# RWKV block and cross attention on one core: first quarter mixed chunk by chunk, v's weights centred later, one signal per swap, two weights loaded later

## The reference, cut to what matters

```python
xa = _ln(x, ln1_w, ln1_b)
sx = concatenate([state[:, 1:2] - xa[:, :1], xa[:, :-1] - xa[:, 1:]], axis=1)
xxx = tanh((xa + sx * maa_x) @ maa_w1).reshape(b, l, 5, DM)      # the low rank, DM = 32
xxx = einsum('blfd,fde->blfe', xxx, maa_w2)
xm = xa[:, :, None] + sx[:, :, None] * (maa_stack + xxx)         # five mixes: k, w, v, r, g
xk, xw, xv, xr, xg = (xm[:, :, j] for j in range(5))
w = exp(-exp(time_decay + tanh(xw @ td_w1) @ td_w2))
r, k, v = xr @ Wr.T, xk @ Wk.T, xv @ Wv.T;  g = silu(xg @ Wg.T)
# a scan over the 128 steps: out = r (u * k v + s); s = k v + w * s
# per-head norm of out: subtract the mean over the head's 16 columns, divide by the deviation
x1 = x + og * g @ Wo.T                                            # then a feed-forward part
```

## Time and profile before

| | |
|---|---|
| runs | 951.91, 955.3, 957.22 us; median 955.3 us |
| profiled execution | 953.33 us, span in the trace 951.6 us |
| busy share of the span | TensorE 92%, VectorE 72%, GpSimd 56%, ScalarE 41% |
| mean granted TensorE clock | 0.965 of full speed |
| moved by DMA | 100.34 MB, 105 GB/s |

### The profile page before, as it was taken

How to read it: one execution, slowest core, us unless ns; L and a number is a source line. 1 busy time by engine, 2 the same in 40 slices (tenths; PEclk the granted TensorE clock), 3 DMA queues, 4 the chain that set the end, 5 groups by cost and what they waited for, 6 DMA issues and landing times.

```text
span 951.6 us, 10578 instructions
## 1 busy us (share of the span) xinstructions
PE 877.9 (92%) x3588; PEld 392.8 (41%) x3588; DVE 688.8 (72%) x875; ACT 388.2 (41%) x755; POOL 535.4 (56%) x573
## 2 busy tenths in 40 slices
PE   2789999999989997999899998999979999799988
PEld 1234433443434442444344444444435444444454
DVE  6336799899879996889889999779995324523442
ACT  3032323332234322213235454554446353736394
POOL 1001685888949789399789996888873101010200
PEclk8698999999979998899999999999989999999999
DMA  8082458465773639265734043446002212010101
GB/s 288 11 169 86 122 145 167 143 177 138 155 185 113 186 80 196 70 171 147 208 106 112 24 105 103 109 109 163 17 23 67 78 33 79 0 45 1 44 1 44
DMA packets 93943, 100.34 MB, mean 105 GB/s; under 512 B 22850, under 2 KB 64066, under 8 KB 91842
## 3 DMA queue, kind: packets, MB, share of 16 engines
q1 hardware_dynamic: 86978, 87.09, 36.3%
q10 hardware_dynamic: 6912, 12.59, 3.8%
HBM read 65.05 MB, written 33.55 MB: 104 GB/s over the span
## 4 chain that ended last, share of the span: by engine, by line
PE 54%; DVE 16%; POOL 10%; issue 6%; ACT 5%; DMA 4%; SPq 3%; ACTq 0%; DVEq 0%; POOLq 0%
PE PS L1359 36%; PE PS L1488 3%; DVE M L1072 3%; DVE VB L1188 3%; PE PS L1592 3%; POOL VB L755 3%; PE PS L1368 3%; POOL VB L751 2%; POOL VB L747 2%; PE PS L1426 2%; PE PS L1569 2%; DMA scr_v<-STG 2%; DVE VB L1069 2%; SPq L497 2%; PE PS L1503 1%
## 5 line engine op out<-in xcount | busy, mean ns | idle before, releaser
L1359 PE MATMUL PS<-M,W 128*128 128x512 f32 x544 | 264.4, 628 | 15.5 <-DVE M L1072 11.6
L1359 PEld LDWEIGHTS PS<-M,W 128*128 128x128 f32 x544 | 102.4, 199 | 154.2 <-issue 138.1
L747 POOL TENSOR_TENSOR VB<-KR,VB 128x1008 f32<-128x1008 f32 x64 | 129.8, 2028 | 58.0 <-PE PS L1488 53.3
L1188 DVE TENSOR_TENSOR_SCAN VB<-PS,VB 128x512 f32<-128x512 f32 x128 | 149.0, 1206 | 16.1 <-POOL VB L755 14.2
L755 POOL TENSOR_TENSOR VB<-VB 128x1008 f32<-128x1008 f32 x64 | 151.1, 2362 | 3.5
L1069 DVE TENSOR_TENSOR VB<-VB,PS 128x2048 f32<-128x2048 f32 x64 | 146.0, 2282 | 2.0
L635 POOL TENSOR_SCALAR NM<-MV 128x2 f32<-128x2 f32 (+1 forms) x24 | 5.4, 227 | 231.2 <-DVE MV L1316 141.7
L751 POOL TENSOR_TENSOR VB<-WG,VB 128x1008 f32<-128x1008 f32 x64 | 128.7, 2011 | 0.1
L1359 PE MATMUL PS<-W,M 128*128 128x512 f32 x224 | 105.7, 597 | 0.0
L1334 DVE TENSOR_REDUCE SM<-PS 128x1 f32<-128x512 f32 x64 | 43.4, 687 | 55.7 <-PE PS L1592 55.0
L1488 PE MATMUL PS<-VB,HEAD 128*32 128x512 f32 x512 | 69.7, 617 | 5.2 <-DVE VB L1069 5.0
(11 more groups left out here) (176 smaller groups left out, 1317.8 us busy)
## 6 DMA issues: line engine op xcount, KB each, us to landing
VB<-scr_vs SPq DMA_DIRECT2D x64, 256.0 KB, 7.5
W<-in_w SPq DMA_DIRECT2D x8, 1024.0 KB, 9.2
scr_vs<-STG SPq DMA_DIRECT2D x64, 64.0 KB, 5.1
scr_v<-STG SPq DMA_DIRECT2D x16, 256.0 KB, 6.3
scr_w<-STG ACTq DMA_DIRECT2D x16, 256.0 KB, 5.0
scr_k<-STG ACTq DMA_DIRECT2D x16, 256.0 KB, 2.1
KR<-scr_k SPq DMA_DIRECT2D x16, 256.0 KB, 4.2
WG<-scr_w SPq DMA_DIRECT2D x16, 256.0 KB, 5.6
```

The costliest lines, as they stand in the source:

```text
L747: po.tensor_tensor(vo, KO[:, 0:N2 - 1].unsqueeze(1).to_broadcast([P, S, N2 - 1]), VB[:, 2 + s, 0, :, 1:N2], ALU.mult).then_inc(g_kv, 1)
L1188: sc = dv.tensor_tensor_scan(s_, PS[:, 5, :], b_, 0.0, ALU.mult, ALU.add)
L1359: mm = pe.matmul(o, l, r, start=i == 0, stop=i == 3)
```

## The change

Four edits, and the five order tables written anew for them:

1. In quarter 0 `shift_a` and `first_mix` give way to `front_by_chunk`: for each chunk of 128 channels, as soon as its EXT is there, two subtractions of a quarter of the size and the chunk's first mix.
2. Centring v's weights is a stream of its own ("w", `stream_w`), which the order table puts behind the first mix.
3. Each of the four swaps has its own semaphore `d_xr[f]`, and `mix(q, f)` waits for that of its f alone.
4. The weights of r and g are loaded behind quarter 0's swaps.

```diff
-        d_xr = sem("d_xr")
+        d_xr = [sem(f"d_xr{f}") for f in range(4)]
...
-                for wi in (W_K, W_R, W_G):
-                    sp.dma_start(W[:, wi], w8[wi].rearrange("(c p) n -> p c n", p=P)).then_inc(d_w[wi], 16)
-                    yield
+                sp.dma_start(W[:, W_K], w8[W_K].rearrange("(c p) n -> p c n", p=P)).then_inc(d_w[W_K], 16)
+                yield
                 for q in range(NQ):
...
                     for f in range(4):
-                        sp.dma_start(low_rank(f, 1), low_rank(f, 0)).then_inc(d_xr, 16)
+                        sp.dma_start(low_rank(f, 1), low_rank(f, 0)).then_inc(d_xr[f], 16)
+                        yield
+                    for wi in (W_R, W_G) if q == 0 else ():
+                        sp.dma_start(W[:, wi], w8[wi].rearrange("(c p) n -> p c n", p=P)).then_inc(d_w[wi], 16)
                         yield
...
-            def centre_wv():
+            def stream_w():
...
+            def front_by_chunk():
+
+                w.wait_ge(g_col, 1)
+                sx, xa = SXS[0].rearrange("p c (b t) -> p c b t", t=L), EXTS[0][:, :, :, 1:L + 1]
+                for ec in range(C4):
+                    w.wait_ge(a_ext, ec + 1)
+                    for late, part in ((xa[:, ec, :, EVEN], ODD), (EXTS[0][:, ec, :, 0:N2], EVEN)):
+                        tt(sx[:, ec, :, part], late, xa[:, ec, :, part], ALU.subtract).then_inc(v_sub, 1)
+                    yield
+                    w.wait_ge(v_sub, 2 * (ec + 1))
+                    w.wait_ge(d_vec, 32)
+                    stt(btv(mof(0, None)[:, ec, :]), sxv(ec, 0), vec(V_MX + ec), xav(ec, 0), ALU.mult, ALU.add).then_inc(v_m1, 1)
+                    yield
...
                     if q == 0:
-                        yield from centre_wv()
-                    yield from shift_a(q)
-                    yield from first_mix(q)
+                        yield from front_by_chunk()
+                    else:
+                        yield from shift_a(q)
+                        yield from first_mix(q)
...
-                        w.wait_ge(d_xr, 64 * (q + 1))
+                        w.wait_ge(d_xr[f], 16 * (q + 1))
```

Of the order tables the first rows of one show the kind of edit:

```diff
 ORDER_DVE = (
-    "a:2 end:1 a:17 end:1 m:13 end:1 m:2 end:1 m:6 a:2 m:1 a:1 m:2 a:2 m:1 a:3 m:1 end:1 m:2 l:1 end:1 "
+    "a:16 w:5 m:13 end:1 m:4 end:1 m:4 a:2 m:2 a:4 m:1 a:1 m:1 a:1 m:5 end:2 m:2 end:2 a:6 p:1 scan:6 p:1 "
```

More of the change, by code:

```diff
@@ L1111, in first_mix @@
                 for ec in range(C4):
-                    w.wait_ge(v_sub, 2 * (q + 1))
+                    w.wait_ge(v_sub, 2 * (q + 1) + 6)
                     w.wait_ge(d_vec, 32)
@@ L1344, in stream_l @@
                     yield
-            weave(ORDER_DVE, {"a": stream_a(), "m": stream_m(), "p": stream_p(), "scan": stream_scan(), "end": stream_end(), "c": stream_c(),
+            weave(ORDER_DVE, {"a": stream_a(), "m": stream_m(), "w": stream_w(), "p": stream_p(), "scan": stream_scan(), "end": stream_end(), "c": stream_c(),
                               **{n: stream_l(i) for i, n in enumerate(LANES)}})
```

## The result

The changed kernel takes 932.56 us (median of four runs, 929.47 to 933.27), the kernel before 955.33 on the same chip: ratio 0.9759, 95% interval 0.9723 to 0.9795. Two later series, each on another chip, gave 0.9788 (0.9752 to 0.9824) and 0.9773 (0.974 to 0.9806). So it is 2.1 to 2.4% faster, some 20 to 23 us. I had said 945 us, 10 us faster, between 938 and 952: the gain was more than twice what I forecast, and outside the range. Two single executions in the experiments, of 4959 and 3072 us, stood far from all others of their kernels and are in no ratio.

A forecast was written before the change was run, and what follows sets the result against it. The prediction took TensorE, busy 92% of the span, with its holes and halved clock, as the bound. Front 8.1 plus stores 1.0 made 9.1 us off 953.3: 944.2 (946.2 from the median), stated as 945 us, range 938 to 952.

The forecast's parts named there:

- The front: Quarter 0's start: chunked first mix, later centring and swap signals let VectorE start on a mix result 8.1 us sooner (7.4 to 8.9).
- The stores of v: Ahead of the projection of k: earlier issue and faster landing of the last store gain 1.0 us, bounds 0 and 2.7.
- The weights of r and g: Loaded behind quarter 0's swaps, they should land by 32 us, in idle DMA time, at no cost.
- The clock's rival: Projections from 37.03 to 46 us at full instead of half clock: 4.5 us more gain, some 940 us; chance 0.15.
- All the rest of the five tables: Order tables beyond the priced terms: same instructions in another order, mostly by a few places; taken as 0.
- for one crowded queue: Quarter 3's store of v landing in 11.90 us: TensorE's wait plus work lost to the halved clock, priced at 11 us.
- a second such stall in quarter 1: X2's 1 MB load ahead of quarter 1's first scr_v store gives the gain back: 955 us, no change; chance 0.13.
- my sign that no hole behind 100 us would be longer than quarter 3's: TensorE, behind 100 us: no hole longer than the 6.04 us of quarter 3.
- My other sign: Quarters 1 to 3: ScalarE's longest wait for a store of v stays at or below 6.4 us.

The follow-up runs named there:

- one seam: Changed kernel with the old order tables from quarter 4's projections, near 420 us, on; against the kernel before: ratio 0.9861 (0.9826 to 0.9897).
- another run with a seam: Changed kernel with each engine's table new up to the end of quarter 2's projections and old behind; against the kernel before: ratio 1.0022 (0.9996 to 1.0048).

## Why the prediction was wrong

**The front was right.** The last first mix ended at 19.94 us (19.9 forecast), the low rank at 21.13 (21.2), the mix began at 23.94 (23.9), VectorE took its result at 26.05 (26.1). The gain at this point is 34.20 - 26.05 = 8.15 us, 8.1 forecast. The first projection gained 7.65 (37.03 to 29.38), since it now waits 0.72 us for ScalarE's WOB: rows of the weights WL were put ahead of it. The eight differences of 256 elements took 0.42 us each (417 to 425 ns) where I took 0.41; two of them overlap a little, 0.76 us from the start of the first to the end of the second. The formula of the Trainium skill, "VectorE: DVE Perf Modes", section on the trn2 errata, gives 0.42 as an estimate, and the trace agrees.

**The stores of v were mis-sized.** "I take 0.55 + 0.45 = 1.0 us": the last store of v was issued 3.18 us after its copy instead of 3.71, which is the 0.55, but it landed after 4.6 us instead of 4.24. The hole ahead of the projection of k stayed, 2.33 for 2.26 us. So this term gave 0.2 net, and the projection of k came at 63.9 and not at 62. The weights of r and g landed at 30.1 and 33.0 us, the second 1 us later than I had said, at no cost that the trace shows.

**The clock's rival did not come.** The projections of v still ran at the low level (halved clock from 24.0 to 37.6 us, before from 32.5 to 46.2). What went was another stretch, 18.9 to 25.7 us under the low rank; I had allowed for a part of it in the low rank's time.

**The step that failed** is "All the rest of the five tables: the same instructions in another order, mostly by a few places. I take 0". The edits with the old tables gave 0.9912, 8.4 us, and my sum was 9.1, so the forecast is that of the edits. With the tables it is 0.976 to 0.979, so the other rows are worth 12 to 15 us. I priced this term at nothing without going through the holes that those rows could close, and the trace of before has two large ones behind the start.

The one at quarter 2's decay (4.17 us, then 10.3 us of halved clock in which TensorE was busy for 9.87) stands in none of my sums; by the way I priced quarter 3's it is 4.17 + 4.9 = 9 us. It is here that the result's trace gains most, 10.6 us from 246 to 287, and 10.1 and 11.1 in the other two; with the edits alone it was 1.4. Up to 3.6 us of that can be the one trace of before, as said above.

The other is quarter 3's store of 11.90 us. I had priced it at 11 us "for one crowded queue", and moving four rows out of that queue in the kernel before measured 10.5 us in the trace. But I used the price only to ask whether the change makes a second such stall in quarter 1, and never asked whether the new order removes the one that is there. It does so in part: the slowest store took 9.7, 9.4 and 7.3 us in the three traces of the changed kernel, TensorE's hole of 6.04 us is gone and one of 2.40 us, for GpSimd, stands there, and the lead grows by 3.8, 5.5 and 8.8 us from 287 to 405.

The new rows also cost something that I had not priced: the wait ahead of the feed-forward's first mix is 6.72 us instead of 4.51. That is longer than 6.04, so my sign that no hole behind 100 us would be longer than quarter 3's failed. My other sign, that ScalarE's waits for a store of v stay below 6.4 us, was met, with 3.17 at most.

**What stays open.** SyncE's rows for quarter 2's stores to 440 us account for 7 of the 12 to 15 us on one chip. With SyncE's whole table old nearly all was lost (0.9899), although its rows ahead of quarter 2 counted for nothing by themselves (0.9776); the two ran on different chips, and how much of it is interplay I can't say. Which of the new rows close the hole at quarter 2's decay is open: with SyncE's old table 7.9 us of lead came there still, so the computing engines' rows have a part. SyncE's new rows over old rows of the other engines weren't tried, so what they are worth alone is open. Whether the 1 MB load of X counts (0.9992, 0.9828, 0.9875) is not settled, nor is a kernel with the four edits, the old tables and only the four rows moved, which wasn't tried: 0.9912 x 0.9845 = 0.976 is an estimate from two runs, if their gains add, no better than the changed kernel.

## What to carry to other kernels

When a change rewrites an order of work, go through every stall that the profile of before shows, not only the place of the edit, and ask of each whether the new order removes it; a price that was read for a feared stall is as good for one that goes away. Look at what stands in a DMA queue between the stores that a computing engine waits for: reloads put ahead of those stores, into a stretch where the queue had little to do, were worth more here (0.9845) than the rewritten front (0.9912). A piece of a schedule is hard to value by cutting it in: one seam cost 4.5 us of lead, and another run with a seam came out at 1.0022, though the edits alone gave 0.9912; moving a few rows in one queue left the order of all other engines as it was. And before a gain at one place of one trace is believed, look at the same place in a trace of a program that is the same up to there.

## What was unexpected

- The third store of v in quarter 3, 256 KB, took 3.9 us to land when the seven reloads of 256 KB stood ahead of all four stores (the others 7.7, 6.3 and 3.7). With them in between, the third took 10.3 to 12.6 us in the kernel before and in the nine experiments that kept SyncE's order there, and 8.6 in the run that put them back. The four DMAs of a later store took SyncE 5.27 us to issue instead of 2.51.
- The clock turns small differences into large ones. In the changed kernel TensorE has the same hole of 2.40 us, waiting for GpSimd, near 355 us in each of its three traces. In two of them the clock then stood at 0.56 and 0.76 of full from 360 to 370 us, and the lead grew from 366 to 405 us by 1.9 and 3.5 us; in the third it stayed at 1.00, and the lead grew by 6.7. What followed the same hole thus differed by 5 us between executions of one program.
- Two traces of programs that are the same up to 286 us differ by 7 us at 287: in one ScalarE waits 4.06 us for a store of v and TensorE 3.21, in the other TensorE has no such hole.
- One signal for each swap cut a wait of TensorE by 1.9 us, and the program came out 5 us faster (2 to 8). The trace doesn't show what the rest comes from.
